# Squares moved to ScalarE, attention weights turned by plain transposes and scaled afterwards, and four order lists redrawn, in a two-layer transformer kernel on one core

## The reference, cut to what matters

```python
# layer 0
ada = silu(cond) @ Wada.T + bada                  # gamma1, gamma2, scale1, scale2, shift1, shift2
qkv = (ln(x) * (scale1 + 1) + shift1) @ Wqkv.T + qkv_bias
qn = q / max(norm(q), 1e-12) * sm                 # norms: a sum of squares for each head
kn = k / max(norm(k), 1e-12)
o = softmax(qn @ kn.T + attn_bias) @ v
x = x + (o @ Wproj.T + bproj) * gamma1
h = gelu_tanh((ln(x) * (scale2 + 1) + shift2) @ Wfc1.T + bfc1)
x = x + (h @ Wfc2.T + bfc2) * gamma2
# layer 1
h = rms_norm(x) * (cond @ norm_w.T + 1)
q, k, v = split(h @ qkv_w.T)
q, k = q * sqrt(scale) * rsqrt(sum(q*q) + eps), k * sqrt(scale) * rsqrt(sum(k*k) + eps)
q, k = rope(q), rope(k)
o = softmax(where(mask, q @ k.T, -1e30)) @ v
out = o @ out_w.T + x
```

## Time and profile before

| | |
|---|---|
| median of 3 runs | 251.08 us (249.48 to 252.08) |
| time of the profiled execution | 250.84 us |
| its span, first to last instruction | 249.1 us |
| busy: PE, DVE, ACT, POOL | 233.1, 211.3, 144.5, 113.3 us |
| mean granted TensorE clock over the span | 0.986 |

### The profile page before, as it was taken

How to read it: one execution, slowest core, us unless ns; L and a number is a source line. 1 busy time by engine, 2 the same in 40 slices (tenths; PEclk the granted TensorE clock), 3 DMA queues, 4 the chain that set the end, 5 groups by cost and what they waited for, 6 DMA issues and landing times.

```text
span 249.1 us, 5057 instructions
## 1 busy us (share of the span) xinstructions
PE 233.1 (94%) x1840; PEld 179.9 (72%) x1840; DVE 211.3 (85%) x422; ACT 144.5 (58%) x288; POOL 113.3 (45%) x183
## 2 busy tenths in 40 slices
PE   6899999999997999989999999999998599999992
PEld 2569575666675667557699999999895486876882
...
DMA packets 3642, 9.76 MB, mean 39 GB/s; under 512 B 536, under 2 KB 920, under 8 KB 3360
## 3 DMA queue, kind: packets, MB, share of 16 engines
q1 hardware_dynamic: 3616, 9.41, 10.6%
...
## 4 chain that ended last, share of the span: by engine, by line
PE 70%; DVE 14%; issue 6%; POOL 3%; ACT 3%; DMA 3%; SPq 0%; DVEq 0%; ACTq 0%
PE ring L813 9%; PE ring L807 9%; PE ring L809 8%; PE ring L808 8%; PE ring L1087 6%; PE psx L946 6%; PE pv L916 5%; PE ring L870 5%; DVE nm L1192 4%; PE pv L1102 3%; PE psx L896 3%; PE psx L1077 3%; DVE xh L1175 2%; DMA qstk<-stage_a 1%; DVE bnst L1157 1%
## 5 line engine op out<-in xcount | busy, mean ns | idle before, releaser
L1192 DVE TENSOR_REDUCE nm<-ring 128x2 f32<-128x512 f32 x64 | 40.4, 684 | 3.9 <-PE ring L870 3.5
L624 ACT ACTIVATE ps<-psx 128x1024 f32<-128x1024 f32 x32 | 31.3, 1026 | 8.6 <-PE psx L896 8.6
L470 POOL TENSOR_TENSOR rstd<-ve,half_neg 128x2 f32<-128x2 f32 x12 | 8.5, 711 | 34.8 <-DVE ve L1161 28.3
L807 PE MATMUL ring<-wqkv_hi,xm_hi 128*128 128x512 f32 (+1 forms) x64 | 23.5, 367 | 0.0
L946 PE MATMUL psx<-ident_b 128*128 128x512 bf16 x66 | 21.3, 450 | 2.0 <-POOL ones L465 2.0
L809 PE MATMUL ring<-wqkv_hi,xm_lo 128*128 128x512 f32 (+1 forms) x64 | 21.6, 337 | 0.0
L808 PE MATMUL ring<-wqkv_lo,xm_hi 128*128 128x512 f32 (+1 forms) x64 | 21.6, 337 | 0.0
L723 ACT ACTIVATE ps<-ring,col 128x256 f32<-128x256 f32 x32 | 13.4, 476 | 12.9 <-PE ring L809 12.3
L870 PE MATMUL ring<-kstk,qstk 64*128 64x256 f32 x128 | 18.6, 328 | 1.3 <-DVE nm L1192 1.3
L870 PEld LDWEIGHTS ring<-kstk,qstk 64*128 64x128 f32 x128 | 12.2, 191 | 9.3 <-DVE nm L1192 5.0
L514 POOL TENSOR_TENSOR qn<-qk 128x512 f32<-128x512 f32 x8 | 8.6, 1078 | 22.6 <-DVE stack L1337 14.9
...
## 6 DMA issues: line engine op xcount, KB each, us to landing
...
```

The lines of the kernel that those rows point to most:

```text
L624: a.activation(ps[:, n % 4], psx[:, n % 2], ACT.Exp).then_inc(exp_done, 1)
L807: mm(dst, lhs[0], rhs[0], start=start, stop=False)
L1192: v.tensor_reduce(nm[:, :, par, p], bank(key).rearrange("p (q n) -> p q n", q=TB), AX.X, ALU.max, negate=True).then_inc(ring_dve, 1)
```

## The change

1. `square0` and `square1` leave POOL's list and become ScalarE activations (function Square), one for each tile, 16 in all, with the same waits as before.
2. `diag1` becomes `inv1`: the reciprocal alone. `turnp1` on PE is a transpose of the unnormalised weights and no longer waits for DVE. New: `spread1` (ACT copies each reciprocal over 64 columns, 128x256, into `spread`), `turninv1` (PE transposes the spread reciprocals of a batch, four transposes, into a ring bank; ACT copies it into `o_raw`), `heads1_scaled` (DVE multiplies `pv` by it into `at`). `heads1` and `heads1_lo` then read `at`.
3. SP's order becomes a list, `SYNC_ORDER`: Wfc1 is loaded ahead of `shift0:0`, Wfc2 behind `shift0:2`.
4. The constants of POOL get semaphores of their own, and the four lists are redrawn. The number of filler steps stays at 33.

```diff
+SYNC_ORDER = steps("""
+load_w1 shift0:0 shift0:1 shift0:2 load_w2 shift0:3 load_wqkv1 load_wout1 proj1:0 proj1:1 proj1:2 proj1:3
+""")
...
-stats0:0 silu norm0:0 ada split_wqkv0:0 split_wqkv0:1 split0:0 stats0:1 stats0:2 norm0:1 qk0:0.0 qk0:0.1
+stats0:0 silu norm0:0 ada split_wqkv0:0 split_wqkv0:1 split0:0 stats0:1 qk0:0.0 norm0:1 head_scales qk0:0.1
...
+    if name == "turninv1":
+        return [(("iT", b), "act")]
...
-        diag = o_raw[:, :, :].rearrange("p s (h n) -> p s h n", h=H1)
+        spread = o_raw[:, 0, :].rearrange("p (t f n) -> p t f n", t=TB, f=FC)
...
-                if name == "square0":
-
-                    t = TB * b + i_
-                    pool.wait_ge(*emptied(("qk", t)))
-                    if t >= TB:
-                        pool.wait_ge(stk_hi, t - TB + 1)
-                        pool.wait_ge(stk_lo, t - TB + 1)
-                    g.tensor_tensor(qn[:, t % TB, :], qk[:, t % TB, :], qk[:, t % TB, :], ALU.mult)\
-                     .then_inc(sq_ready, 1)
...
+                if name == "square0":
+
+                    t = TB * b + i_
+                    act.wait_ge(*emptied(("qk", t)))
+                    if t >= TB:
+                        act.wait_ge(stk_hi, t - TB + 1)
+                        act.wait_ge(stk_lo, t - TB + 1)
+                    a.activation(qn[:, t % TB, :], qk[:, t % TB, :], ACT.Square).then_inc(sq_ready, 1)
+                if name == "square1":
+
+                    t = TB * b + i_
+                    if t >= TB:
+                        act.wait_ge(*full(("T1", t - TB)))
+                    act.wait_ge(*emptied(("qk1", t)))
+                    a.activation(qn[:, t % TB, :], qk[:, t % TB, :], ACT.Square).then_inc(sq1_ready, 1)
...
+                if name == "spread1":
+
+                    m = 2 * b + i_
+                    act.wait_ge(inv1_ready, m + 1)
+                    if b >= 1:
+                        act.wait_ge(*full(("iT", b - 1)))
+                    else:
+                        act.wait_ge(*full(("oT", B - 1, 0)))
+                    a.activation(spread[:, i_, :, :].rearrange("p f (i n) -> p f i n", i=2),
+                                 inv1[:, m % 2, :].rearrange("p (i f) -> p f i", i=2).unsqueeze(3)
+                                 .to_broadcast([P, FC, 2, D1]), ACT.Copy).then_inc(spread_ready, 1)
+                if name == "turninv1":
+                    act.wait_ge(*full(("iT", b)))
+                    if b >= 1:
+                        act.wait_ge(heads1_scaled, b)
+                    else:
+                        act.wait_ge(*full(("oT", B - 1, 1)))
+                    a.activation(o_raw[:, 1, :], bank(("iT", b)), ACT.Copy).then_inc(ring_act, 1)
                 if name == "heads1":
-                    act.wait_ge(pv_full, 4 * B + b + 1)
+                    act.wait_ge(heads1_scaled, b + 1)
...
                         pe.wait_ge(exp_done, PAIRS * B + m + 1)
-                        pe.wait_ge(diag_ready, m + 1)
                         for kc in range(TB):
                             dst = claim(("P1", b, i_, kc))
-                            for h in range(H1):
-                                last = mm(dst[:, h * P:(h + 1) * P], weights_q[m % 2][:, h % 2, h // 2, kc * P:(kc + 1) * P],
-                                          diag[:, m % 2, h, :], start=True, stop=True)
-                            last.then_inc(ring_full, 1)
+                            transposes(dst, [weights_q[m % 2][:, h % 2, h // 2, kc * P:(kc + 1) * P]
+                                             for h in range(H1)]).then_inc(ring_full, 1)
+                    if name == "turninv1":
+
+                        dst = claim(("iT", b))
+                        pe.wait_ge(spread_ready, 2 * b + 2)
+                        transposes(dst, [spread[:, qc, f, :] for f in range(FC) for qc in range(TB)])\
+                            .then_inc(ring_full, 1)
...
-                if name == "diag1":
+                if name == "inv1":
...
-                    step(v.reciprocal(inv1[:, m % 2, :], sums1[:, m % 2, :]))
...
+                    v.reciprocal(inv1[:, m % 2, :], sums1[:, m % 2, :]).then_inc(inv1_ready, 1)
...
+                if name == "heads1_scaled":
+                    dve.wait_ge(pv_full, 4 * B + b + 1)
+                    dve.wait_ge(*emptied(("iT", b)))
+                    if b >= 1:
+                        dve.wait_ge(heads1_hi, b)
+                        dve.wait_ge(at_ready, B + b)
+                    v.tensor_tensor(at[:, :, :].rearrange("p f n -> p (f n)"), pv[:, :], o_raw[:, 1, :], ALU.mult)\
+                     .then_inc(heads1_scaled, 1)
```

More of the change, by code:

```diff
@@ L86 @@
[L86 to L88 removed]
+qk0:0.1 busy:12 normed0:1 ada_rest busy:13 v0:0 busy:14 v0:1 busy:15 qk0:1.0 qk0:1.1 normed0:2 gamma_rows
+busy:16 turnq0:0.0 busy:17 turnk0:0.0 turnq0:0.1 gamma:0 flag busy:18 turnk0:0.1 busy:32 gamma:1 branch max0:0.0
@@ L101 @@
[L101 to L104 removed]
+normed1:1 score0:3.6 score0:3.7 out0:3.0 proj0:2 value0:3.2 value0:3.3 fc1:0.0 fc1:0.1 fc1:0.2 out0:3.1 fc1:0.3
@@ new lines @@
+heads0:3 fc1:1.0 fc1:1.1 proj0:3 normed1:2 fc1:1.2 fc2:0 fc1:1.3 fc1:2.0 fc1:2.1 normed1:3 fc1:2.2 fc1:2.3
+normed2:0 fc2:1 qk1:0.0 fc1:3.0 qk1:0.1 fc1:3.1 fc2:2 fc1:3.2 fc1:3.3 v1:0 normed2:1 fc2:3 normed2:2 qk1:1.0
+turn1:0.0 qk1:1.1 turn1:0.1 v1:1 score1:0.0 score1:0.1 normed2:3 qk1:2.0 turn1:1.0 qk1:2.1 v1:2 turn1:1.1
+turnp1:0.0 score1:1.0 turnp1:0.1 score1:1.1 turninv1:0 value1:0 qk1:3.0 turn1:2.0 qk1:3.1 turn1:2.1 v1:3
+turnp1:1.0 score1:2.0 turnp1:1.1 score1:2.1 value1:1 turn1:3.0 turninv1:1 turnp1:2.0 turn1:3.1 proj1:0
@@ L105 @@
+score1:3.0 turnp1:2.1 turninv1:2 score1:3.1 value1:2 turnp1:3.0 proj1:1 turnp1:3.1 turninv1:3 value1:3 proj1:2
+proj1:3
 """)
 VECTOR_ORDER = steps("""
-stats0:0 silu norm0:0 ada split_wqkv0:0 split_wqkv0:1 split0:0 stats0:1 stats0:2 norm0:1 qk0:0.0 qk0:0.1
-head_scales sums0:0 bias_count split0:1 ada_rest norm0:2 v0:0 flag stats0:3 unit0:0.0 v0:1 qk0:1.0 lo0:0.0
-unit0:0.1 qk0:1.1 lo0:0.1 gamma_rows sums0:1 split0:2 norm0:3 max0:0.0 max0:0.1 max0:0.2 unit0:1.0 max0:0.3
-lo0:1.0 unit0:1.1 qk0:2.0 max0:0.4 lo0:1.1 qk0:2.1 max0:0.5 max0:0.6 sums0:2 max0:0.7 neg0:0 split0:3 shift0:0
@@ L122 @@
-heads1_lo:0 rsums1:3 diag1:1.1 max1:2.0 turnp1:1.0 turnp1:1.1 rope:3.0 rope:3.1 diag1:2.0 proj1:0 max1:2.1
-diag1:2.1 turnp1:2.0 max1:3.0 heads1_lo:1 turnp1:2.1 max1:3.1 diag1:3.0 proj1:1 diag1:3.1 heads1_lo:2 turnp1:3.0
-turnp1:3.1 proj1:2 heads1_lo:3 proj1:3
+stats0:0 silu norm0:0 ada split_wqkv0:0 split_wqkv0:1 split0:0 stats0:1 qk0:0.0 norm0:1 head_scales qk0:0.1
+stats0:2 sums0:0 bias_count split0:1 ada_rest norm0:2 v0:0 stats0:3 unit0:0.0 v0:1 qk0:1.0 unit0:0.1 lo0:0.0
+qk0:1.1 lo0:0.1 gamma_rows norm0:3 split0:2 flag sums0:1 max0:0.0 max0:0.1 max0:0.2 max0:0.3 unit0:1.0 unit0:1.1
@@ new lines @@
+qk0:2.0 lo0:1.0 max0:0.4 lo0:1.1 qk0:2.1 max0:0.5 max0:0.6 sums0:2 max0:0.7 neg0:0 split0:3 shift0:0 split_wproj
+max0:1.0 max0:1.1 unit0:2.0 max0:1.2 unit0:2.1 qk0:3.0 max0:1.3 lo0:2.0 max0:1.4 qk0:3.1 max0:1.5 max0:1.6
+max0:1.7 lo0:2.1 neg0:1 out0:0.0 shift0:1 sums0:3 out0:0.1 max0:2.0 max0:2.1 max0:2.2 unit0:3.0 max0:2.3
+unit0:3.1 v0:2 max0:2.4 max0:2.5 max0:2.6 lo0:3.0 max0:2.7 neg0:2 heads0_lo:0 lo0:3.1 shift0:2 proj0:0 stats1:0
+out0:1.0 max0:3.0 max0:3.1 max0:3.2 norm1:0 max0:3.3 max0:3.4 max0:3.5 out0:1.1 max0:3.6 max0:3.7 neg0:3
@@ new lines @@
+gelu:2.1 gelu:2.2 normed2:0 gelu:2.3 split_wout1 qk1:0.0 square1:0.0 fc1:3.0 qk1:0.1 square1:0.1 fc1:3.1
+gelu:3.0 gelu:3.1 fc1:3.2 gelu:3.2 fc1:3.3 gelu:3.3 v1:0 normed2:1 normed2:2 qk1:1.0 turn1:0.0 square1:1.0
+qk1:1.1 turn1:0.1 square1:1.1 v1:1 exp1:0.0 normed2:3 qk1:2.0 exp1:0.1 turn1:1.0 qk1:2.1 v1:2 turn1:1.1
+square1:2.0 square1:2.1 spread1:0.0 turnp1:0.0 spread1:0.1 turnp1:0.1 turninv1:0 exp1:1.0 qk1:3.0 turn1:2.0
+square1:3.0 qk1:3.1 turn1:2.1 square1:3.1 exp1:1.1 v1:3 turnp1:1.0 heads1:0 turnp1:1.1 spread1:1.0 spread1:1.1
@@ L152 @@
+stats2:3 root1:1 cos:2.0 cos:2.1 root1:2 cos:3.0 cos:3.1 root1:3
 """)
```

166 lines of the change are left out of this document (72 added, 94 removed).

## The result

The changed kernel takes 244.34 us in the median of 4 runs (242.82 to 246.39), the kernel before 250.94 (249.48 to 252.08, 4 runs): a ratio of 0.974, 95% interval 0.970 to 0.979. The forecast was 242.7 us, in a range of 239.0 to 248.0. The profiled execution took 244.30 us, its span 242.4.

What follows compares the result with a forecast made beforehand. PE was taken as the bound from 55 us on, DVE next, with DVE setting the pace before. Terms +1.2 - 2.7 - 1.9 - 2.9 - 3.2 + 1.4 = -8.1 took 250.84 to 242.7 us, range 239.0 to 248.0.

Steps and rivals of the forecast that it cites:

- A: Start of the kernel: `stats0:2`, moved on DVE, delays the sums and POOL's root; +1.2 us, bounds 0 to +2.0.
- 0.77 reaches the root: Start: 1.44 us of moved statistics, less 0.67 us of DVE wait regained, delays POOL's root by 0.77 us.
- B: Shift of batch 1: PE's 1.21 us DMA wait and 1.5 us lost to low clock go; -2.7 us, bounds -3.3 to -1.0.
- the part from 125 us on: Between 125 and 181 us: PE is busy 55.05 of 56 us with the same work; 0 us.
- C: Start of second attention: squares on ACT bring batch 1's root and DVE's rope earlier; -1.9 us, bounds -2.5 to -0.7.
- both reach it: Start of second attention: root's gain (about 1.0 us) and rope's (0.85) both shorten PE's 3.37 us of waits; -1.9 us.
- D: 199.5 to 224 us: PE saves 3.5 by transposes, DVE 2.9 without diagonals; smaller counts, -2.9 us, bounds -4.0 to -1.0.
- E: 224 us to the end: four `turnp1` gain, new steps cost, last wait is filled; -3.2 us, bounds -4.5 to -1.5.
- hand-offs: Second attention: ACT's added squares, spreads and copies delay exponents or copies PE waits for; +1.4 us, bounds 0 to 4.7.
- the refill of the last wait: Before the last projection: batch 2's projection, now behind the last `value1`, fills PE's 1.42 us wait; -1.4 us.
- ACT isn't the bound: Rival, second attention: ACT's added work becomes the bound, costing 4.7 us in place of 1.4; 246.0 us, chance 0.10.
- The clock did not fall with the transposes: Rival, second attention: with transposes and more waits PE's granted clock falls to the lower level; 253.3 us, chance 0.04.

Runs made afterwards that it cites:

- second measurement: The same changed kernel, unaltered, measured once more beside the kernel before: median 242.84 us against 250.77, ratio 0.969.
- late `cos`: Changed kernel with POOL's first `cos` product of batch 2 held back until DVE finished the last rope of batch 1: median 243.01 us.
- Two buffers: Changed kernel with high and low parts of the second attention's outputs in two buffers in turn: median 243.13 us.

## Why the prediction was right, step by step

The direction holds, and the sum (-8.1) is 1.4 too large against the profiles' -6.7 and close to the second measurement's -7.9. Not every term came about as it was argued, and that the sum is this near is in part luck. By its terms:

**A, +1.2.** The stretch grew by 1.48, of which 0.4 is the clock, and the part before it shrank by 0.25: the size is near, the place is not. The step that failed is "0.77 reaches the root": `unit0:0.0` starts at 26.08, not 0.7 to 1.2 later. The 0.67 in it was read wrongly, since `norm0:1` belongs to batch 1 and the second `qk0`, of batch 0, is not made from it. And the gain of the squares on ACT, left out of the value, does reach the root: DVE's sums start 0.32 us later, but the second of them no longer waits 0.48 us for POOL's square. DVE's rows before, then after:

```profile
17.91 0.68 DVE L1316 TENSOR_REDUCE ss<-qn 128x32 f32<-128x512 f32 x1
19.07 0.69 DVE L1316 TENSOR_REDUCE ss<-qn 128x32 f32<-128x512 f32 x1 [0.48 <-POOL qn L514]
```

```profile
18.23 1.27 DVE L1347 TENSOR_REDUCE ss<-qn 128x32 f32<-128x512 f32 x2
```

The loss comes behind `unit0`: PE's first `max0` starts 11.2 us after it (10.8 in the four profiles without the low clock), where it was 9.9. That DVE's waits make it was tried and fell; what else among PE's list, ACT's copies and the branch does is open, since both other edits of that stretch made it longer.

**B, -2.7.** Alone it is -2.2, so the reading of the earlier trace rows was right and the term 0.5 too large. Inside the change the stretch gained 1.88 in all, because the mask's new place takes 1.2 back; the prediction had given POOL's moved steps no price. About 0.9 of gain is left that no run assigns; it lies between the first `score0` and `normed2:2`, of which the prediction had the part from 125 us on at 0.

**C, -1.9.** Measured -1.73. The root of batch 1 starts 189.28 - 181.40 = 7.88 us behind `normed2:2` before and 187.68 - 180.75 = 6.93 after, 0.95 earlier, as forecast. But "both reach it" was right only in part. Of PE's three waits, 3.37 us together, 0.48 and 1.17 are left and the third is gone. With the squares back on POOL the first two are 0.86 and 1.59, and the stretch is 0.6 longer; the third stays away. PE's new list has the twelve products of `v1:2` ahead of that turn, where they stood behind it:

```profile
195.06 0.28 PE L835 MATMUL ring<-wqkv_hi,xm_hi 128*128 128x256 f32 x1
...
196.50 0.60 PE L841 MATMUL ring<-ident,qn 128*128 128x128 f32 x4
```

So some 0.6 of the 1.73 is the squares, and by subtraction about 1.1 the redrawn list, for which the prediction had no term; a run that moves `v1:2` alone is missing. The second half of C was wrong as a mechanism: the rope of 1.26 us was to be 0.42 again with the square gone, and is 1.52, because a `cos` product stands there now. The late `cos` shows that this slot was worth only 0.2.

**D, E and hand-offs, -4.7.** Measured -4.59 + 0.27 = -4.32. The transposes cost 1.06 us for eight (1.07 forecast), the spreads 0.43 each (at most 0.63). The step of E that failed is the refill of the last wait, -1.4: PE waits 1.50, since `at_hi` is free only when the refilling projection has read it. Two buffers bring 0.9. The 1.4 kept back for hand-offs makes up for it, since none of the waits that the profile lists for PE in the second attention names ACT; that the two sizes agree is luck. Nor does the sum hold because PE's 8 us arrive: in the kernel before, without any new step, only 4 of them do, and new waits for the ropes take 2.1 of the rest. In the change the squares on ACT shorten those waits, which is worth 2.3 from the first `turnp1` on by the run that undoes it; what the redrawn lists add there was not separated.

**The rivals.** ACT isn't the bound (17.99 of 24.5, and no listed wait of PE there names it). The clock did not fall with the transposes: it is 1.00 in 199.5 to 224, where five `turnp1` run, and falls only at 240.9 us, when PE has ended. So the sentence of the Trainium skill, "TensorE: Matmul & The Clock Gate", Part 4, by which the full clock does not engage for transposes, is not borne out here.

ACT's and POOL's busy time were forecast at 160 and 95 us, and are 156.6 and 95.3. The last rope ends at 219.5 us, 4.7 before its old place, where 5 to 7 were forecast.
